# Two transformer layers on one NeuronCore: scale rows loaded ahead of two weights, a shorter warm-up, and side jobs of TensorE in pairs behind chosen maxima

## What is computed

```python
x = x + L0_attn(layernorm(x))   # 16 heads of 16, biases, ALiBi, causal mask
x = x + L0_ffn(layernorm(x))    # int weights: W = (wq - 128) * scale; down(silu(gate) * up), 704 hidden
x = x + L1_attn(layernorm(x))   # 16 heads of 16, weights transposed, causal mask
x = x + L1_ffn(layernorm(x))    # weights rounded to fp8; 768 hidden, a scale per output column
```

## Time and profile before

| | |
|---|---|
| median of three runs | 439.06 us (438.38 to 439.29) |
| the profiled execution | 439.59 us |
| its span (first to last instruction) | 437.9 us |
| granted TensorE clock, mean | 0.992 |
| busy: TensorE, VectorE, ScalarE, GpSimd | 410.4, 300.3, 233.9, 170.5 us |
| bytes moved by DMA | 22.97 MB |

### The profile page before, as it was taken

One profiled execution on the slowest core, in us unless ns is written; L12 is line 12 of the kernel. 1 busy time (PEld: TensorE's weight loads), 2 busy tenths in 40 slices (PEclk: granted clock), 3 DMA queues, 4 the chain that ended last, 5 costly groups with the idle time before them and its releaser, 6 DMA issues.

```text
span 437.9 us, 14535 instructions
## 1 busy us (share of the span) xinstructions
PE 410.4 (94%) x6328; PEld 234.6 (54%) x6328; DVE 300.3 (69%) x604; ACT 233.9 (53%) x377; POOL 170.5 (39%) x250
## 2 busy tenths in 40 slices
PE   5899989999999988999999998998999999899997
PEld 5456654455555346544476465544545553475476
DVE  5545899999997127511335668999999971278883
ACT  3644456677677854212101641565786779545950
POOL 5118323202202236296881000235262553353870
PEclk9999999999999999999999997999999999999999
DMA  7799540000000000202000577400000000000002
GB/s 209 126 247 290 136 114 4 4 3 4 4 3 4 4 1 6 73 0 73 1 0 0 146 196 200 115 3 4 4 2 4 4 5 2 2 1 0 2 29 69
DMA packets 21657, 22.97 MB, mean 52 GB/s; under 512 B 2588, under 2 KB 20858, under 8 KB 21594
## 3 DMA queue, kind: packets, MB, share of 16 engines
q1 hardware_dynamic: 20498, 19.03, 17.0%
q0 software_dynamic: 544, 2.49, 1.9%
q10 hardware_dynamic: 552, 0.53, 0.4%
HBM read 8.27 MB, written 1.05 MB: 21 GB/s over the span
## 4 chain that ended last, share of the span: by engine, by line
PE 71%; DVE 15%; ACT 4%; DMA 3%; issue 2%; POOL 2%; SPq 2%; ACTq 0%; DVEq 0%
PE ps L777 11%; PE ps L757 11%; DVE mx L1250 11%; PE ps L735 10%; PE ps L908 8%; PE ps L1004 5%; PE ps L936 4%; PE ps L913 4%; ACT prob L1133 4%; PE ps L972 4%; PE ps L669 3%; DMA col_rows<-in_L_ffn_up_scale 3%; PE ps L836 3%; PE ps L743 2%; POOL xn L592 1%
## 5 line engine op out<-in xcount | busy, mean ns | idle before, releaser
L1250 DVE TENSOR_REDUCE mx<-ps 128x1 f32<-128x512 f32 (+3 forms) x304 | 182.1, 654 | 24.7 <-PE ps L743 22.0
L1133 ACT ACTIVATE prob<-ps 128x1024 f32<-128x1024 f32 (+1 forms) x192 | 146.0, 812 | 75.4 <-PE ps L757 73.5
L735 PE MATMUL ps<-kS,qS 99*32 99x512 bf16 (+20 forms) x1536 | 114.1, 321 | 4.7 <-DVE mx L1250 2.7
L577 POOL TENSOR_SCALAR_AFFINE_SELECT prob<-prob 128x256 f32<-128x256 f32 x128 | 52.0, 412 | 163.3 <-ACT prob L1133 161.9
L757 PE MATMUL ps<-qS,kS 101*32 101x512 bf16 (+7 forms) x1536 | 97.0, 328 | 3.7 <-ACT prob L1133 3.6
L777 PE MATMUL ps<-prob,v 128*32 128x512 f32 (+3 forms) x768 | 80.1, 488 | 0.6 <-POOL prob L577 0.4
L735 PEld LDWEIGHTS ps<-kS,qS 99*32 99x32 bf16 (+1 forms) x1536 | 43.7, 95 | 53.1 <-DVE mx L1250 29.0
L757 PEld LDWEIGHTS ps<-qS,kS 101*32 101x32 bf16 (+1 forms) x1536 | 35.2, 96 | 32.4 <-ACT prob L1133 14.9
L740 PE MATMUL ps<-mask_q,identb 128*32 128x32 bf16 (+1 forms) x1024 | 52.0, 186 | 0.0
L743 PE MATMUL ps<-mask_q,identb 128*32 128x64 bf16 (+1 forms) x512 | 46.2, 198 | 0.0
L740 PEld LDWEIGHTS ps<-mask_q,identb 128*32 128x32 bf16 x1024 | 28.8, 98 | 11.0 <-issue 6.4
(11 more groups left out here) (144 smaller groups left out, 548.9 us busy)
## 6 DMA issues: line engine op xcount, KB each, us to landing
qS<-parts SPq DMA_DIRECT2D x24, 128.0 KB, 3.1
kS<-parts SPq DMA_DIRECT2D x24, 128.0 KB, 3.1
qS<-prob SPq DMA_DIRECT2D x12, 128.0 KB, 6.2
kS<-prob SPq DMA_DIRECT2D x12, 128.0 KB, 5.9
qS<-xn SPq DMA_DIRECT2D x12, 128.0 KB
kS<-xn SPq DMA_DIRECT2D x12, 128.0 KB
out<-x SPq DMA_DIRECT2D x8, 128.0 KB, 1.7
oT<-in_L_ffn_gate_w POOLq DMA_DIRECT2D x1, 768.0 KB, 4.8
```

Source lines behind the costliest of these rows:

```text
L577: nc.gpsimd.affine_select(out=square, in_=square, compare_op=ALU.is_ge, fill=0.0, base=0, pattern=[[0, 2], [1, P]], channel_multiplier=-1) ...
L735: mmi = nc.tensor.matmul(span[r:r + STRIP, 0:seen], qS[0:K_MAX[L], c, g * G + h, qt * P + r:qt * P + r + STRIP], kS[0:K_MAX[L], g * G + h, ...
L1133: nc.scalar.activation(prob[:, n % 3, 2 * pair:2 * pair + 2, off:CH], ps[:, 2 * (m % 2):2 * (m % 2) + 2, off:CH], ACT.Exp, scale=SCALE).th ...
L1250: ins = nc.vector.tensor_reduce(mx[:, slot, qt, heads[0]:heads[-1] + 1, part], src, AX_X, ALU.max)
```

## The change

The eight row loads move ahead of `Wv` and `Wo`. The two ALiBi loads move from SP's queue to GpSimd's, between its first and its second `rstd_of`. The warm-up has 26 products instead of 60, and six more stand behind the turning of the first four tiles. One v projection less runs ahead of the first layer's maxima (`V_FIRST` 4 instead of 5). Side jobs no longer stand behind each maximum but in twos: in the first layer behind maxima whose number modulo 7 is 1, 3 or 5, which are 1, 3, 5, 8, 10, 12, 17, 19 and 22 (number 15 is a turn); in the second behind those whose number modulo 6 is 3, which are 3, 9 and 21, until the layer's jobs are done (`N_SIDE`).

```diff
-WARM = 60
+WARM = 26
+WARM_QK = 6
 COLS_BEFORE = 4
-V_FIRST = (5, 2)
+V_FIRST = (4, 2)
+SIDES_BEHIND = ((1, 3, 5), (3,))
+SIDES_PERIOD = (7, 6)
+SIDES_AT_ONCE = 2
+N_SIDE = (NT + HT + HT // 2 + 4, NT)
@@ sync
-            for m, n in ((2, "Wv"), (3, "Wo")):
-                sp.dma_start(w0[:, m], a[f"L0_attn_{n}"].rearrange("(j p) o -> p j o", p=P)).then_inc(wvo_in, 16)
             full = HID0 // P
-            sp.dma_start(k_chunks[QK_ROWS:K_EXP[0]], tail[0:ALIBI_ROWS[0] + MAX_ROWS, :, 0:CH]).then_inc(tail_in, 16)
-            sp.dma_start(q_chunks[QK_ROWS:K_MAX[0]], tail[ALIBI_ROWS[0] + MAX_ROWS:, :, 0:CH]).then_inc(tail_in, 16)
             sp.wait_ge(rows_zero, 1)
...
                 sp.dma_start(col_rows[row:row + whole.shape[0]], whole).then_inc(rows_in, 16)
+            for m, n in ((2, "Wv"), (3, "Wo")):
+                sp.dma_start(w0[:, m], a[f"L0_attn_{n}"].rearrange("(j p) o -> p j o", p=P)).then_inc(wvo_in, 16)
             sp.dma_start(bo[:], a["L0_attn_bo"].unsqueeze(0).to_broadcast([P, C])).then_inc(bo_in, 16)
@@ gpsimd
             rstd_of(0)
+            pool.dma_start(k_chunks[QK_ROWS:K_EXP[0]], tail[0:ALIBI_ROWS[0] + MAX_ROWS, :, 0:CH]).then_inc(tail_in, 16)
+            pool.dma_start(q_chunks[QK_ROWS:K_MAX[0]], tail[ALIBI_ROWS[0] + MAX_ROWS:, :, 0:CH]).then_inc(tail_in, 16)
             rstd_of(1)
@@ tensor, attention
-                        if ("exp", 0, 0) in ORDER[n_entry:]:
-                            side_job(L, side)
-                            side += 1
+                        if side < N_SIDE[L] and (m_n - L * N_MAX) % SIDES_PERIOD[L] in SIDES_BEHIND[L]:
+                            for _n in range(SIDES_AT_ONCE):
+                                side_job(L, side)
+                                side += 1
@@ tensor, start
                 ln_transposes("xnT", 2 * L, 0, L, take_a, a_full)
+                for _n in range(WARM_QK if L == 0 else 0):
+                    nc.tensor.matmul(ps[:, 7, 0:P], identb[:], mask_q[:], start=True, stop=True)
```

More of the change, by code:

```diff
@@ L785, in attention @@
                 ready = set()
-                for n_entry, entry in enumerate(ORDER):
+                for entry in ORDER:
                     if entry[0] == "max":
```

## The result

The changed kernel takes **443.07 us** (median of 12 executions, 438.83 to 445.74), the kernel before took 439.12 beside it (12 executions, 437.81 to 442.56). The ratio is 1.0064, 95% interval 1.0039 to 1.0089: slower, where 435.8 us was forecast. The ratio leaves out executions in a slow state, here the one of 445.74 us, and is not the quotient of the two medians (1.0090). The profiled execution took 439.95 us (span 438.2) and is one of its fastest; two more executions were profiled later, since this one doesn't show all that the median holds.

The account below looks back on a forecast made before the run. Bounds: a start waiting for a load, TensorE work behind it, then VectorE's maxima. Terms -3.6 + 0.6 - 0.3 = -3.3 us took the profiled 439.59 to 436.3, the median 0.53 lower: 435.8 us, range 433.0 to 438.4.

Parts of the forecast that it names:

- The head: Start of the kernel: shorter warm-up and earlier scale rows let q/k product 4 start at 17.45 instead of 21.04, 3.6 us less.
- rivals on the start's clock: Start: TensorE stays at 1.2 GHz for a while, 437.6 us, chance 0.15; or through products 0 to 3, 442.8, chance 0.04.
- on Wo: Start: Wo, now loaded last, lands at 20.8 or later, so the head gives nothing before it; 439.4 us, chance 0.07.
- The wait for the scale rows: Start: TensorE stands from near 19.4, the end of product 3, until the transpose of the scale rows at 20.89.
- so what is gained ahead of product 4 stays: After the start: from 21.04 products and v projections run back to back, so the head's gain of 3.6 us lasts.
- nothing waits on it: SP's stacking behind the start: it moves up by about 2 us, and nothing waits on it before the exponentials.
- The first layer's side jobs: First layer's attention: pairing saves 0.54 us on TensorE but adds two waits; sum +0.6 us, bounds -0.5 and +1.6.
- Projection 4 leaves a hole that cost nothing: Ahead of the first layer's maxima: projection 4 filled a free hole, so pairing projections 4 to 7 costs +0.65 us.
- The drained banks: First layer: the first exponential waits until ScalarE has drained every bank behind the last side job, +0.74 us.
- The second layer: Second layer's attention: paired side jobs gain 1.1 us, the clock falls and may catch a pair; -0.3 us taken.
- the worse bound: Second layer: the pair behind maximum 21 is caught whole at 1.2 GHz, making that layer's term +0.9 us.
- The slower one: Start: the clock stays low through q/k products 0 to 3, which take 7.0 us more; 442.8 us, chance 0.04.

Follow-up runs that it names:

- before_adds_late: Kernel before, with only GpSimd's eight bias adds moved one by one behind triangle cuts 8 to 15: 439.8 us, ratio 0.9989.
- before_adds_twice_look2: Kernel before, with GpSimd's eight bias adds made twice, a second execution of it: 445.34 us, beside 441.18 for the kernel before.
- after_l1_old: Changed kernel, with the second layer's side jobs one behind each maximum as before: 442.76 us, ratio 1.0055 to the kernel before.
- after_down_early: Changed kernel, with the first feed-forward's down weight loaded right behind gate and up: 439.01 us, ratio 0.9958 to the kernel before.
- after_adds_late_v5_warm60: Changed kernel, with late GpSimd adds, five projections first, 60 warm-up products and none behind the first transposes: 437.68 us, ratio 0.9961.
- after_adds_late_v5_down_early: Changed kernel, with late GpSimd adds, five projections first and the down weight loaded right behind gate and up: 438.81 us, ratio 0.9964.
- after_adds_late_v5: Changed kernel, with GpSimd's adds moved behind triangle cuts and five projections instead of four ahead of the first layer's maxima: 438.71 us, ratio 0.9965.
- loads_only: Kernel before, with only the diff's loads moved, warm-up and side jobs as before: 439.02 us, ratio 0.9966.
- after_adds_late_v5_l1_old: Changed kernel, with late GpSimd adds, five projections first and the second layer's side jobs one by one: 438.24 us, ratio 0.9967.

## Why the prediction was wrong

**The head: right.** 3.72 us against 3.6 in the profiled execution, 2.9 and 3.2 in the two others (product 4 at 18.10 and 17.82, against 21.04); warm-up 2.95 us; issues on GpSimd's queue 0.94 and 0.70 us, with room; no wait of product 2, 4 or of the column transpose; the rows for the maxima landed 11.7 us after their issue, long before their use. The rivals on the start's clock and on Wo (landed in 4.5 us) didn't come about. The wait for the scale rows was priced too low, by its length alone: it took 1.17 to 2.27 us in the four profiles that have it, and behind the two longest (before_adds_late, before_adds_twice_look2) the clock was at 0.50 for 2 us and more.

**The step that failed: "so what is gained ahead of product 4 stays".** It followed TensorE and VectorE through the earlier trace rows and took the other engines' work to move with them. SP's queue did move by 2 us, as I said, but I read "nothing waits on it" for the parts and forgot the weights it issues between them, whose issues moved with it. Their landing, GpSimd's dequantisation and its adds stay; the first maxima and side jobs ran into them. One prediction row showed a neighbour of it: GpSimd's issue at 41.35 in the earlier trace rows stands between dequantisation and adds, whose rows I hadn't read. In the changed kernel this costs, by execution: the negation up to 4.8 us, TensorE's wait for the down weight 0 to 2.1 us, for the maxima's small DMA up to 3.2 us. Late adds or an earlier down weight take the slowdown away, each clear of its interval, which shows that the collision with GpSimd's work made the change slower. They don't bring the forecast's 3.3 us: the best version (0.9958) is 1.8 us below the kernel before.

*The Trainium skill, "SBUF — State Buffer" (SBUF: two separate sides), has VectorE and GpSimd share a pair of ports, which one of them holds alone for a whole instruction while the other stops fully; on VectorE's side only some kinds of instruction need it. The trace agrees with the exclusion (0.18 us alone, 0.52 to 4.80 beside the adds), and shows more: the wait lasted over up to seven adds of 0.69 us. I weighed that section only against GpSimd's two DMA issues, where nothing came of it, and not against GpSimd's arithmetic.*

**The first layer's side jobs: +0.6 forecast, +3.94 in the profile.** "Projection 4 leaves a hole that cost nothing": the hole was 0.81 us ahead of that projection in the kernel before and is 1.81 now, and in the profiled execution the clock fell in it; the pair behind took 3.37 instead of 1.99 us, VectorE waited 3.20. In the second and third execution the clock held there and fell behind the later, longer holes. Late adds with five projections instead of four made 0.9999 into 0.9965; the intervals overlap, so this share is likely and not settled. Over all versions, the clock fell there in four of the seven profiled executions with four projections first (hole of 1.8 us) and in none of the thirteen with five (0.8 us). The drained banks cost 0.68 us (the row at 54.19) where I said 0.74. A pair of transpose jobs came to 0.59 + 0.43 = 1.02 us in the sum; the first three took 1.03, 1.22 and 1.07 in the chain.

**The second layer: -0.3 forecast, +0.1 in the profile**, inside its bounds. The clock fell and caught the pair, as the worse bound had it, and one by one it is no faster (after_l1_old, 1.0055).

**The range.** Its low end takes 0.9 us for the side jobs' low bound, which lies 1.1 below their term (+0.6 to -0.5), so it should have been 432.8; this changes nothing here.

**The rivals.** None held the mechanism. The slower one had the right currency, TensorE's clock, in the wrong place: between dense products at the start instead of behind waits in the attention. A rival "GpSimd's work doesn't move, the maxima run into it" could be had from two rows, the dequantisation's wait for the load at 39.73 and the adds at 42.17, and 3.6 us subtracted from 46.53.

**What stays open.** The shares of the three stops in the median's 4 us: late adds alone give 0.65% and the earlier down weight alone 1.06%, and together with five projections no more than either, so they overlap. Why the negation is let in after one add in one execution and after seven in another wasn't found. That the weights' loads take longer because the stacking of q/k parts starts earlier is read from the windows; the short warm-up brings it on, but the stacking wasn't moved by itself. What TensorE waits for in the holes inside a maximum (1.40 to 2.30 us in four profiled executions) isn't known, nor why the 2 us of the short warm-up never reach the end.

**The best version** is not told apart among six: after_down_early 0.9958, after_adds_late_v5_warm60 0.9961, after_adds_late_v5_down_early 0.9964, after_adds_late_v5 0.9965, loads_only 0.9966, after_adds_late_v5_l1_old 0.9967. Each beats both kernels by its interval, and loads_only is the smallest edit.

## What to carry to other kernels

When a start is shortened, list every engine's work of the next stages and ask of each what starts it: what hangs on a load's landing or on another queue's pace doesn't move, and what does move runs into it. Small operations of VectorE beside a row of GpSimd arithmetic had no fixed price here, so keep the two apart by order. And TensorE's idle holes ahead of dense work can cost twice, by their length and by the clock behind them.

## What the hardware showed that was not expected

- A VectorE operation of 0.18 us took 0.52 to 4.80 us beside eight GpSimd adds of 0.69 us each, in one and the same program 0.74 and 4.52 us.
- TensorE's clock went to 1.2 GHz behind a hole of 1.81 us in one execution and held behind the same hole in two others; the low stretches in the first layer then lasted some 3 to 10 us.
- Loads issued 2 us and more earlier took 2.5 us longer (6.2 to 8.7 us for 704 KB) when the DMA engines' share rose from 0.82 to 1.13.
- TensorE stood 1.40 to 2.30 us ahead of the same mask product in four profiled executions, where the program waits for nothing, with GpSimd's adds beside it or not.
- Twelve executions of one kernel differ by 4.8 us (before) and 6.9 us (changed) of 440, and the changed kernel spends 10 to 18 us of an execution at 1.2 GHz.
